# Vision block on one Trainium2 core: unturned scores first, an earlier second layer norm for two groups, second queries in 222 and 370 columns, key copies on ScalarE

## The reference, cut to what matters

```
h = tokens(x)                       # ternary weights, 8-bit activations, 768 -> 256, class token, position
h = h + attention(layernorm(h))     # 16 heads of 16
h = h + experts(layernorm(h))       # 8 heads of 64, 8 experts per head, top 1

attention: q, k, v = split(x @ Wqkv);  q_rot, k_rot = rotate(q), rotate(k)
  num = exp(q_rot . k_rot / 4)                   # turned
  den = sum(exp(q . k / 4))                      # unturned, over all keys
  y   = (causal(num) / den) @ v;  return y @ Wout + bout
experts:   q = x @ w_q; k = x @ w_k; gates = sigmoid(x @ w_gate)
  each token and head takes its best expert for values and for output; causal softmax attention
```

## Time and profile before

| | |
|---|---|
| median of 3 runs | 241.33 us (240.1 to 242.55) |
| the profiled execution's own time | 240.91 us |
| its span in the profile | 238.4 us |
| mean granted clock of TensorE | 0.979 |
| TensorE busy (matmuls) | 207.9 us, 87% |
| VectorE, ScalarE, GpSimd busy | 178.7, 93.7, 79.5 us |

### The profile page before, as it was taken

How to read it: one execution, slowest core, us unless ns; L and a number is a source line. 1 busy time by engine, 2 the same in 40 slices (tenths; PEclk the granted TensorE clock), 3 DMA queues, 4 the chain that set the end, 5 groups by cost and what they waited for, 6 DMA issues and landing times.

```text
span 238.4 us, 5151 instructions
## 1 busy us (share of the span) xinstructions
PE 207.9 (87%) x2079; PEld 179.6 (75%) x2079; DVE 178.7 (75%) x324; ACT 93.7 (39%) x184; POOL 79.5 (33%) x82
## 2 busy tenths in 40 slices
PE   0153969689979799999999999999999999999994
PEld 0033849688865689987677777778989999999993
DVE  1679895998977767933558666775799979979972
ACT  3578739958741335445332155156202022110000
POOL 8562677000443424002253564955661000000000
PEclk9999999979999679999999999999999999999999
DMA  6998000000000010001602006067005435532102
GB/s 177 265 302 322 2 0 4 0 3 3 3 3 3 18 71 3 0 0 29 252 3 88 3 12 254 0 181 201 3 7 185 120 123 172 165 95 61 44 0 103
DMA packets 7181, 19.56 MB, mean 82 GB/s; under 512 B 1043, under 2 KB 1878, under 8 KB 7030
## 3 DMA queue, kind: packets, MB, share of 16 engines
q1 hardware_dynamic: 7158, 19.24, 26.3%
HBM read 18.55 MB, written 0.68 MB: 81 GB/s over the span
## 4 chain that ended last, share of the span: by engine, by line
PE 49%; DVE 28%; issue 9%; ACT 4%; POOL 4%; DMA 4%; SPq 1%; DVEq 0%; ACTq 0%; POOLq 0%
PE ps L265 13%; PE ps L266 11%; PE ps L267 11%; DVE gx L1101 7%; DMA tw<-tok_weight 4%; PE ps L1233 3%; PE ps L1274 2%; PE ps L1434 2%; DVE oelo L1075 2%; DVE rden L930 2%; DVE amax L774 1%; PE ps L1404 1%; ACT ptb L720 1%; DVE stat L803 1%; POOL velo L485 1%
## 5 line engine op out<-in xcount | busy, mean ns | idle before, releaser
L1101 DVE TENSOR_TENSOR gx<-maskb,oT 128x1184 fp32r<-128x1184 bf16 x31 | 42.3, 1414 | 0.6 <-PE ps L267 0.6
L1038 DVE COPY_PREDICATED v<-onehot,ps 128x512 f32<-128x512 uint8 (+3 forms) x40 | 25.7, 661 | 17.6 <-PE ps L267 17.3
L265 PE MATMUL ps<-gx,oelo 128*128 128x296 f32 x124 | 37.8, 305 | 0.6 <-DVE gx L1101 0.6
L267 PE MATMUL ps<-gx,oehi 128*128 128x296 f32 x124 | 37.2, 300 | 0.0
L266 PE MATMUL ps<-gx,oehi 128*128 128x296 f32 x124 | 37.0, 298 | 0.0
L265 PE MATMUL ps<-vehi,x2lo 128*128 128x512 f32 (+3 forms) x90 | 35.2, 392 | 0.0
L266 PE MATMUL ps<-velo,x2hi 128*128 128x512 f32 (+3 forms) x90 | 33.3, 370 | 0.0
L267 PE MATMUL ps<-vehi,x2hi 128*128 128x512 f32 (+3 forms) x90 | 33.2, 369 | 0.0
L485 POOL TENSOR_TENSOR velo<-veraw,vehi 128x1024 fp32r<-128x1024 f32 x8 | 19.1, 2390 | 23.8 <-ACT vehi L657 17.3
L265 PEld LDWEIGHTS ps<-gx,oelo 128*128 128x128 f32 x124 | 23.3, 188 | 1.8 <-issue 1.3
L266 PEld LDWEIGHTS ps<-gx,oehi 128*128 128x128 f32 x124 | 23.4, 189 | 0.0
(11 more groups left out here) (165 smaller groups left out, 479.8 us busy)
## 6 DMA issues: line engine op xcount, KB each, us to landing
maskb<-mask_rows SPq DMA_DIRECT2D x32, 148.0 KB, 3.9
veraw<-value_w SPq DMA_DIRECT2D x8, 512.0 KB, 3.7
oeraw<-output_w SPq DMA_DIRECT2D x8, 512.0 KB, 4.0
xp<-x_rows SPq DMA_DIRECT2D x6, 336.0 KB, 9.9
w2raw<-w_qkgate SPq DMA_DIRECT2D x1, 1088.0 KB, 14.1
tw<-tok_weight SPq DMA_DIRECT2D x1, 768.0 KB, 8.4
wqraw<-w_qkv SPq DMA_DIRECT2D x1, 768.0 KB, 12.0
out<-yo SPq DMA_DIRECT2D x4, 148.0 KB, 1.9
```

The lines of the kernel that those rows point to most:

```text
L265: pe.matmul(o, llo, rhi, start=start, stop=False)
L267: return pe.matmul(o, lhi, rhi, start=False, stop=stop)
L1038: dve.copy_predicated(v2[0:m, t, h0:h1], bcast(onehot[0:m, t, h0:h1, e], 2, DH2), ps[0:m, JBANK[n], 0:(h1 - h0) * DH2].rearrange("p (a b) ...
L1101: dve.tensor_tensor(gx[:, k % NGR].rearrange("p a b t -> p a (b t)"), bcast(maskb[:, w % NMR, k % MEU], 1, 2), oT[:, c % 2].bitcast(F32), ...
```

## The change

- **Order of the scores.** In batch 0 TensorE makes the unturned scores first, then the turned ones, then jobs 10 and 11 and the sums of batch 0. A function `unit(b, kind)` gives the new order of the sets. ScalarE's order follows: it reads eight jobs, makes its first key copies, reads job 8, then `exps(0, 1)`, more key copies, job 9, `exps(0, 0)`, jobs 10 and 11. In batch 1 `attend(0)` stands between the two sets, and in batch 3 `out_proj(0)` and `out_proj(1)` do.
- **Key copies.** The two masked copies of the turned keys go from VectorE's `rope` to ScalarE's `keys_turned(r)`, which reads `ropet` in SBUF. `RSTEPS` falls from 8 to 6. TensorE's turned scores wait for `krot_ready`; `rope(2)` and `rope(3)` wait until their buffer has been read.
- **Second layer norm.** Output projections 0 and 1 need only two batches now (`OP_AFTER`), with banks given anew (`OPB`, `DENB`). VectorE takes residual, layer norm and low part of groups 0 and 1 ahead of the reciprocals of batches 2 and 3; the other four groups follow. TensorE: `attend(3)`, turns 0 and 1, two `qk2` jobs, the sums of batch 3, output projections 2 and 3, and so on (`D_ORDER`).
- **Second queries and keys.** Columns 0 to 221 (two groups, six images) and 222 to 591 instead of twice 296. Jobs 0 to 7 wait for two groups of `x2lo`; their banks are 7, 0, 1 in turn (`QKB`).
- **GpSimd.** `w2_lo(0)` and `w2_lo(1)` wait for the first two `rope`s, the others for `causal(0)` and `causal(1)`; `ve_lo(0)` for two groups of `x2lo`.
- `ed` and `yo` take other places in SBUF.

```diff
-        RSTEPS = 8
+        RSTEPS = 6
+        def unit(b, kind):
+            return 2 * b + (kind if b else 1 - kind)
...
+        EARLY = 2
+        FRONT = EARLY * R
+        QKT = [slice(0, FRONT), slice(FRONT, T)]
+        NQ2 = 2 * C2
+        QKB = [(7, 0, 1)[n % 3] for n in range(NQ2)] + [4 + n % 4 for n in range(NQ2)]
+        OPB = [(7, 0), (7, D), (4, 0), (4, D), (6, 0), (6, D)]
+        OP_AFTER = [2, 2, 3, 3, NB, NB]
+        DENB = [5, 7, 5, 5]
+        D_ORDER = [("pv", NB - 1), ("turn", 0), ("turn", 1), ("qk", 0), ("qk", 1), ("den", NB - 1), ("out", 2), ("out", 3),
+                   ("qk", 2), ("qk", 3), ("out", 4), ("out", 5), ("qk", 4), ("turn", 2), ("qk", 5), ("qk", 6),
+                   ("turn", 3), ("qk", 7), ("gate", 0), ("gate", 1), ("turn", 4), ("gate", 2), ("turn", 5),
+                   ("qk", 8), ("gate", 3), ("qk", 9), ("gate", 4)]
+        D_ORDER += [("qk", n) for n in range(10, 2 * NQ2)]
...
+            for n in range(2):
+                pool.wait_ge(sm["rope_t"], RSTEPS * (n + 1))
+                w2_lo(n)
+            pool.wait_ge(sm["en_ready"], 2)
+            w2_lo(2)
             pool.wait_ge(sm["en_ready"], 2 * 2)
...
+            def keys_turned(r):
+                hf, c = r // KC, r % KC
+                act.wait_ge(sm["keys_zero"], 2)
+                act.wait_ge(sm["rope_t"], RSTEPS * r + 4)
+                src = ropet[:, r % 2, 1].rearrange("p (i s) -> p i s", s=SE)[:, :, 0:S]
+                for j in range(2):
+                    ins = act.activation(krot[:, c, hf * B // 2:(hf + 1) * B // 2, DH2 * j:DH2 * j + S], src, ACT.Copy,
+                                         scale=cols("par")[:, j:j + 1])
+                ins.then_inc(sm["krot_ready"], 1)
+            for n in range(NPJ - 3):
                 proj_read(n)
+                if n == NPJ - 5:
+                    keys_turned(0)
+            exps(0, 1)
+            keys_turned(1)
+            proj_read(NPJ - 3)
+            exps(0, 0)
+            proj_read(NPJ - 2)
+            proj_read(NPJ - 1)
+            keys_turned(2)
...
+                if b:
+                    exps(b, 0)
+                    if b == 1:
+                        keys_turned(3)
+                    exps(b, 1)
...
-                for j in range(2):
-                    many(dve.tensor_scalar(krot[:, c, im, DH2 * j:DH2 * j + S], tmp[:, 1], cols("par")[:, j:j + 1],
-                                           None, ALU.mult))
...
             residual(0)
             residual(1)
             ln_apply(1, 0)
-            residual(2)
             ln_apply(1, 1)
             x2_lo(0)
+            x2_lo(1)
+            denominators(2)
+            normalise(2)
+            denominators(3)
+            normalise(3)
+            residual(2)
             ln_apply(1, 2)
-            x2_lo(1)
+            residual(3)
             x2_lo(2)
-            denominators(NB - 1)
-            normalise(NB - 1)
-            residual(3)
             ln_apply(1, 3)
             residual(4)
+            x2_lo(3)
             residual(5)
             ln_apply(1, 4)
-            x2_lo(3)
             ln_apply(1, 5)
             x2_lo(4)
             x2_lo(5)
...
             for b in range(NB):
-                scores(b, 0)
                 if b == 0:
+                    scores(0, 1)
+                    scores(0, 0)
                     proj_job(NPJ - 2)
                     proj_job(NPJ - 1)
+                    denominators(0)
+                    continue
+                scores(b, 0)
+                if b == 1:
+                    attend(0)
                 else:
                     denominators(b - 1)
+                if b == NB - 1:
+                    for g in range(EARLY):
+                        out_proj(g)
                 scores(b, 1)
-                if b == NB - 1:
-                    out_proj(0)
-                    out_proj(1)
-                    denominators(b)
-                    for g in range(2, NOP):
-                        out_proj(g)
-                attend(b)
+                if b < NB - 1:
+                    attend(b)
```

More of the change, by code:

```diff
@@ L217, in vit_block @@
         qk.close()
+        yo = sbuf(last, "yo", [P, KC, 2, HALF])
         NOR, NOE = 4, 2
@@ L486, in ve_lo @@
                                    ALU.subtract).then_inc(sm["velo_ready"], 1)
-            for g in range(GI):
+            for g in range(EARLY):
                 rstd_of(1, g)
-            pool.wait_ge(sm["x2lo_ready"], GI)
+            pool.wait_ge(sm["x2lo_ready"], EARLY)
             ve_lo(0)
-            for g in range(GI, G):
+            for g in range(EARLY, G):
                 rstd_of(1, g)
@@ L681, in qk2_evac @@
                 act.wait_ge(sm["qk2_ps"], n + 1)
-                src, col = ps[:, 4 + n % 4, 0:HALF], slice(hf * HALF, (hf + 1) * HALF)
+                col = QKT[hf]
+                src = ps[:, QKB[n], 0:col.stop - col.start]
                 if kind == "k":
@@ L929, in denominators @@
                 dve.wait_ge(sm["den_ps"], b + 1)
[L930 removed]
+                dve.reciprocal(rden[:], ps[:, DENB[b], 0:UN * S]).then_inc(sm["rden_ready"], 1)
             def normalise(b):
@@ L937, in normalise @@
                                   rden[:].rearrange("p (c t) -> p c t", c=KC), ALU.mult).then_inc(sm["yT_ready"], 1)
[L939 to L945, removed]
+            causal(1)
+            denominators(0)
+            normalise(0)
+            causal(2)
+            denominators(1)
+            normalise(1)
+            causal(3)
             def residual(g):
@@ L1322, in qk2_job @@
                 hf, c, kind = QK2[n]
-                if n == 0:
-                    pe.wait_ge(sm["h1_ready"], 2)
-                elif n == 1:
-                    pe.wait_ge(sm["h1_ready"], NOP)
-                elif n < 4:
+                before = [m for m in range(n) if QKB[m] == QKB[n]]
+                if before:
+                    pe.wait_ge(sm["qk2_ready"], before[-1] + 1)
+                elif QKB[n] == 7:
+                    pe.wait_ge(sm["h1_ready"], EARLY)
+                elif QKB[n] < 2:
+                    pe.wait_ge(sm["exp_ready"], 4 * NB)
+                elif QKB[n] == 4:
+                    pe.wait_ge(sm["h1_ready"], 2 * EARLY)
+                elif QKB[n] == 5:
                     pe.wait_ge(sm["yT_ready"], NB)
                 else:
-                    pe.wait_ge(sm["qk2_ready"], n - 3)
+                    pe.wait_ge(sm["h1_ready"], G)
                 base = (NQ if kind == "k" else 0) + c * P
-                tc = slice(hf * HALF, (hf + 1) * HALF)
-                pe.wait_ge(sm["x2lo_ready"], 3 if hf == 0 else G)
+                tc = QKT[hf]
+                pe.wait_ge(sm["x2lo_ready"], G if hf else EARLY)
                 for k in range(KC):
-                    ins = split3(pe, ps[:, 4 + n % 4, 0:HALF], w2hi[:, k, base:base + P], w2lo[:, k, base:base + P],
+                    ins = split3(pe, ps[:, QKB[n], 0:tc.stop - tc.start], w2hi[:, k, base:base + P], w2lo[:, k, base:base + P],
                                  x2hi[:, k, tc], x2lo[:, k, tc], k == 0, k == KC - 1)
@@ L1347, in _ @@
                     out_proj(n)
+                elif kind == "pv":
+                    attend(n)
+                elif kind == "den":
+                    denominators(n)
                 else:
```

77 lines of the change are left out of this document (32 added, 45 removed).

## The result

The changed kernel takes 251.98 us (median, 251.37 to 252.88); the kernel before, with more runs, 240.72 us. The ratio is 1.049, 95% interval 1.043 to 1.055: slower, and far outside the range.

The account below looks back on a forecast made before the run. It took TensorE's stretch up to the first value product, with VectorE's chain ahead of its end, as the bound. New walk 103.2 against old 102.5 gave +0.7 us, so 242.0 us, range 239.0 to 244.6.

Parts of the forecast that it names:

- the interval: TensorE from the last early projection product, 45.57, to the first value product, 102.14: 56.3 us, taken to decide the change.
- The walk: Engine-by-engine timing of old and new queues up to the first value product: 102.5 old, 103.2 new, +0.7 us.
- VP: Start of the first value product on TensorE; predicted at 103.2, between 102 and 104 in the new profile.
- my case of a held clock: TensorE's clock held near 49 and near 76: the walk ends at 100.7, -1.8 us.
- The price of a product of 222 columns: Second queries and keys on TensorE: 0.111 us per product of 222 columns, 0.171 for 370; 0.3 us more over all.
- Rival 2: TensorE's clock falls again ahead of qk2 job 8 or stays down longer: +2.1 to +3.4, 243.4 to 244.7; chance 0.20.
- the clock's: TensorE at half clock for some 3.4 us from 49 and as long again from about 76.
- Rival 1: TensorE's clock holds near 49 and 76: -1.8 us, 239.1 to 239.5; chance 0.20 together with Rival 3.
- Rival 3: ScalarE reaches the second key copies 1.5 us earlier, clock holds: like Rival 1; chance 0.20 for both together.
- Rival 4: 222 columns no cheaper than 296: +0.8 us; a rate several times worse would cost 11 us, 2 in 100.

Follow-up runs that it names:

- the kernel after with filled waits: Kernel after with added dummy products in its waits between the first scores, ahead of attend(1), turns 0 and 1, qk2 jobs 0 and 8: 238.13 us.
- the filled kernels: Dummy products added in waits of the kernel before (237.77 us), the kernel after (238.13 us), and the kernel after without its first part (238.09 us).
- first wait filled: Kernel after with 16 added products ahead of attend(1) alone: 246.32 us over four runs, 243.21 to 248.12.
- other one filled: Kernel after with 16 added products ahead of qk2 job 8 alone: 249.98 us (242.38 to 251.39).
- products behind the wait: Kernel after with 24 added products behind attend(1), not in the wait ahead of it: 250.59 us, ratio 1.042 to the kernel before.
- jobs 10 and 11 moved: Kernel after with projection jobs 10 and 11 between unturned and turned scores of batch 0, no added products: 251.74 us (246.38 to 254.3).
- the second part alone: Kernel after with old score order and key copies back on VectorE; earlier second layer norm and 222/370 columns stay: 243.26 us, ratio 1.013.
- jobs 10 and 11 moved and products added: Kernel after with projection jobs 10 and 11 between the first two score sets and added products in several waits: 238.16 us, ratio 0.992.
- the second part filled: Kernel after without its first part, added products ahead of first scores, around turns 0 and 1, ahead of qk2 jobs 0 and 8: 238.09 us.

## Why the prediction was wrong

**The bound and the interval held.** The first value product moved by 11.3 us and the span by 12.7: later stages followed it nearly one to one. Another 1.4 us were lost behind it, which no run was made to explain.

**The walk held.** The turned scores started at 50.07 (49.8 predicted), 2.54 us behind the unturned ones (2.35); TensorE waited 1.21 us for `causal(1)` (1.3); 1.21 us ahead of job 8 (1.4). ScalarE's two key copies took 0.87 us to its next instruction (0.80, upper end 0.92). `residual(0)` at 78.11 instead of 70.3, and all behind it, came late by the long low stretch: in the kernel after with filled waits, where the clock held there, VP is at 100.4, my case of a held clock being 100.7 (100.3 when put into the trace's frame, in which the walk stood 0.36 too late). In the new order VectorE went from the second low part to the last one in 16.1 us (83.12 to 99.21). I had 17 to 18 and walked with 18.1; the terms that I listed for it add up to 16.3 to 17.7, so that part of the walk was too long by its own numbers.

**The price of a product of 222 columns held**, 0.111 us, and of 370 at 0.17. By the rule of the Trainium skill (TensorE: Matmul & The Clock Gate, LDWEIGHTS) a load of 128 columns of weights takes 107 ns; the trace agrees with it, with 111 ns from one such product to the next at the upper clock.

**Three slips in its sums** changed nothing that was decided here. Products of 222 columns at 0.138 us would have cost 1.3 us more over all 48, and not 0.8. Rival 2's three terms, 0.7, 1.4 and 1.7, add up to 3.8, and not 3.4. And half of 3.73 us for two output projections is 0.93 for one, and not 0.98.

**What failed is one term: the clock's.** I wrote that the forecast "has it at 0.50 for some 3.4 us from 49 on, and once more for as long from about 76", and rival 2 put a third fall at the wait ahead of job 8, "+3.4" at most. Two things were wrong in that. I listed the wait of 1.3 us ahead of `attend(1)` and priced it at its length; rival 2's own point of decision, "about 1 us of wait", would have made it a place to fall, and I applied it only to job 8. And I took the length of a low stretch from rows where it ended soon. Behind 49 us come jobs 10 and 11, 304 columns wide, and even there the same stretch lasted 6.8 us in other runs; behind 61 come three batches of scores, products of 74 and 37 columns. With that stretch at 17.0 us, and the last at 10.2 where I had none or 3.4, the low time is 30.7 us for my 6.8, and half of the 23.9 us more is 12 us.

The miss of VP against the walk is 10.6 us (113.5 less 102.8, my 103.2 put into the trace's frame), and the profile shows where it arose. `residual(0)`, behind the long stretch, is 8.2 us late (78.11 for 69.9 in that frame). VectorE's chain then takes 2.0 us less than walked. From the end of the last low part to VP it is 13.9 us (99.60 to 113.46) for 9.5, 4.4 more, with the stretch of 10.2 us in between.

**The rivals.** Rival 2 had the right side and mechanism, a third fall behind a wait, but the wrong place for the larger one and too small a size. Rival 1 did not occur: the clock held in neither place. Rival 3's early arrival did not occur either, ScalarE reached the second key copies at 48.84, where I had 48.9. Rival 4 is excluded by the 0.111 us.

**The gain that the change was good for.** Its first part removes no wait of TensorE: it puts one set of scores ahead of it and makes another behind. Its second part brings two groups forward and the last one back. Both are draws, as the filled kernels show; but the first put a wait of 1.21 us ahead of `attend(1)`, where the old order had 0.17, and the second one of 1.21 us ahead of job 8, where it had none.

What stays open is when a wait brings the clock down. A wait of 1.21 us ahead of job 0 had a fall within 0.6 us of its end in four kernels (first wait filled, other one filled, products behind the wait, jobs 10 and 11 moved) and none in the kernel after and in the second part alone. Waits of 1.2 us at 48 and 0.9 us at 55 brought none in the kernel with jobs 10 and 11 moved and products added, nor did 1.21 us at 70.4 in the kernel before. It is also open why the last stretch lasts 10.2 us in the kernel after and 6.8 in the second part alone, under much the same products. The runs of some kernels scatter by 5 to 9 us, and their mean clocks with them. I did not test a shorter wait in steps, nor other kinds of added products.

## What to carry to other kernels

Price an idle gap on TensorE by what follows it, not by its length: ask whether the clock may fall there and how long the next work let it stay down where a trace has it at the lower clock. Where a gap of about a microsecond can't be removed, fill it: in these runs 3 to 28 full-width dummy products a gap, put behind the waits that free their bank and in front of the wait itself, cost nothing that could be measured and were worth 1% on the old kernel and 5% on the new one. Compare two orders of work with the clock held before judging the orders.

## What the runs showed of the hardware

- A wait of TensorE made 2.3 us longer cost 8.3 us in all; in the 17 us at half clock behind it TensorE was busy throughout (1.2 GHz for 2.4 GHz, 8.00 of 8.00 us busy in the quoted slice).
- At the lower clock TensorE can be busy without a break and stay there: 17 us in sets of scores, `attend` and sums, and from 99.7 to 109.2 even in products of 64 and 370 columns. In one kernel, 24 bf16 products of 128x128 by 128 columns were followed by the upper clock 3 us after their start.
- The same wait doesn't always bring a fall: 1.21 us ahead of `qk2` job 0 had a fall beside it at 75.6, 83.1, 79.0 and 81.4 in four kernels, and none at 83.65 and 75.55 in two others.
- Added products that took the place of most of a wait of 1.2 us (16 in 1.07 us) kept the clock at 1.00 there in three kernels: all waits filled and first one filled, ahead of `attend(1)`, and the other one filled, ahead of job 8. Ahead of job 8 the clock had already fallen before they began in three kernels (all waits filled, the second part filled, jobs 10 and 11 moved with added products), and it was low for 3.4 us.
- A bf16 product of 128x128 by 128 columns took 0.056 us in a row at the upper clock: 28 of them took 1.74 us and 14 took 0.95, so the 14 more took 0.79.
